# Routing the last two items each by itself, with hand-written order tables for the end of the attention stage

## The reference

```
xc   = x[b] @ W[cat_ids[b]] + b[cat_ids[b]]
x2   = xc + attention(layernorm(xc)) @ Wproj
flat = layernorm(x2)                                # 4096 x 256
gates = softmax(flat @ Wgate)                       # 8 experts
top 2 experts of each token, at most 1024 tokens per expert,
   places given out in the order of the tokens      # a running count
out  = x + x2 + sum over the two experts of gate * (gelu(rows @ W1 + b1) @ W2 + b2)
```

## Time and profile before

| | |
|---|---|
| median of 3 runs | 1525.67 us (1525.51 to 1526.84) |
| the profiled execution | 1527.01 us |
| its span, first to last instruction | 1525.2 us |
| mean granted TensorE clock | 0.957 of full |
| busy share PE, DVE, ACT, POOL | 91%, 68%, 59%, 47% |
| instructions | 27526 |

### The profile page before, as it was taken

One profiled execution on the slowest core, in us unless ns is written; L12 is line 12 of the kernel. 1 busy time (PEld: TensorE's weight loads), 2 busy tenths in 40 slices (PEclk: granted clock), 3 DMA queues, 4 the chain that ended last, 5 costly groups with the idle time before them and its releaser, 6 DMA issues.

```text
span 1525.2 us, 27526 instructions
## 1 busy us (share of the span) xinstructions
PE 1392.3 (91%) x9776; PEld 1221.8 (80%) x9776; DVE 1033.8 (68%) x2435; ACT 906.0 (59%) x2156; POOL 721.4 (47%) x720
## 2 busy tenths in 40 slices
PE   7997699999999999589999999999519999999996
PEld 5876599999999998358778777777419999998996
DVE  2999477777777775567888988895526556556552
ACT  5886255555555543158888888888526546456452
POOL 0788653444344204435465665653252435445333
PEclk9998899999999999689999999999859999999999
DMA  5421256566666614287868678686351343234212
GB/s 171 146 78 37 62 161 181 170 186 180 177 178 186 181 53 123 53 138 139 170 119 165 151 142 172 130 134 104 111 141 21 90 104 95 58 79 100 39 22 28
DMA packets 139449, 182.00 MB, mean 119 GB/s; under 512 B 22486, under 2 KB 107297, under 8 KB 139313
## 3 DMA queue, kind: packets, MB, share of 16 engines
q1 hardware_dynamic: 111152, 128.28, 33.6%
q0 software_dynamic: 28160, 51.96, 16.8%
HBM read 107.28 MB, written 42.08 MB: 98 GB/s over the span
## 4 chain that ended last, share of the span: by engine, by line
PE 78%; DVE 9%; issue 5%; POOL 3%; DMA 2%; ACT 2%; SPq 1%; POOLq 0%; DVEq 0%; ACTq 0%
PE banks L921 50%; PE banks L1365 5%; PE banks L1322 5%; PE banks L1412 3%; PE banks L440 3%; PE banks L983 2%; PE banks L1378 2%; PE banks L1339 2%; DVE lane_at L504 1%; PE banks L1759 1%; PE banks L1426 1%; DVE X L1561 1%; POOL table L1314 1%; PE banks L1346 1%; PE banks L1337 1%
## 5 line engine op out<-in xcount | busy, mean ns | idle before, releaser
L921 PE MATMUL banks<-hi_x,hi_w 128*128 128x320 f32 (+1 forms) x832 | 286.8, 345 | 10.7 <-DVE hidden L956 5.1
L921 PE MATMUL banks<-lo_x,hi_w 128*128 128x320 f32 (+1 forms) x832 | 285.6, 343 | 0.0
L921 PE MATMUL banks<-hi_x,lo_w 128*128 128x320 f32 (+1 forms) x832 | 285.2, 343 | 0.0
L921 PE MATMUL banks<-hi_w,hi_h 128*128 128x256 f32 x896 | 260.2, 290 | 2.1 <-DVE X L1010 1.7
L921 PE MATMUL banks<-lo_w,hi_h 128*128 128x256 f32 x896 | 253.5, 283 | 0.0
L921 PE MATMUL banks<-hi_w,lo_h 128*128 128x256 f32 x896 | 253.5, 283 | 0.0
L863 POOL DMA_INDIRECT xe<-pooled,idx x160 | 156.3, 977 | 198.6 <-PE banks L983 149.2
L1746 POOL DMA_INDIRECT out<-X,tab x64 | 106.5, 1664 | 204.7 <-DVE X L1843 190.1
L1459 ACT ACTIVATE PN<-banks,smax 128x256 f32<-128x256 f32 (+1 forms) x512 | 180.3, 443 | 15.9 <-DVE smax L1553 15.9
L921 PEld LDWEIGHTS banks<-hi_x,hi_w 128*128 128x128 f32 x832 | 158.3, 190 | 24.3 <-issue 10.4
L921 PEld LDWEIGHTS banks<-hi_w,hi_h 128*128 128x128 f32 x896 | 171.2, 191 | 3.3 <-issue 1.3
(11 more groups left out here) (186 smaller groups left out, 3051.4 us busy)
## 6 DMA issues: line engine op xcount, KB each, us to landing
w<-in_L_ffn_w SPq DMA_DIRECT2D x96, 256.0 KB, 5.8
done<-res SPq DMA_DIRECT2D x32, 640.0 KB, 3.9
QS<-parts_qk SPq DMA_DIRECT2D x128, 128.0 KB
KS<-parts_qk SPq DMA_DIRECT2D x128, 128.0 KB, 8.1
BIG<-in_L_ffn_W SPq DMA_DIRECT2D x16, 1024.0 KB, 9.6
mask<-in_c_masks SPq DMA_DIRECT2D x16, 257.0 KB, 2.8
pooled<-XF SPq DMA_DIRECT2D x16, 256.0 KB, 3.2
WS<-in_L_cond_W SPq DMA_DIRECT2D x16, 256.0 KB, 5.7
```

Source lines behind the costliest of these rows:

```text
L921: last = e.matmul(o, a[i], b[j], start=start and k == 0, stop=stop and k == 2, skip_group_check=True)
```

## The change

It does five things. (1) The groups get sizes: `Routing` takes a list, and group 7 is now item 14 alone, group 8 item 15 alone (2 tiles, 4 table writes each); layer 0 keeps 8 groups of 4 tiles. (2) `rounds` runs the tables only up to i = 15, and then a second table per engine, written out by item number (`PE_LAST` and so on). (3) The first two experts' matrices are loaded on SP before the stores of items 14 and 15's last results. (4) ACT and DVE begin to split matrix 0 when their attention work is done, without waiting for the slots, X and the small vectors, and SP loads those vectors ahead of the table. (5) The first product of a unit waits for the first column half alone, and loads of later matrices wait for the transposes of a unit, too.

```diff
-    r1 = Routing(region, "1", E1, K1, 0, CAP1, base1, w_pick1, slot1)
+    r1 = Routing(region, "1", E1, K1, 0, CAP1, base1, w_pick1, slot1, [R] * (NGR - 1) + [TB] * GB)
...
     def act_exp(e, r, g, logits):
-        for q in range(R):
+        for q in range(r.sizes[g]):
...
+    LAST_ROUND = B
+    PE_LAST = (
+        ("scores", 15, 3, 0), ("turn_p", 15, 2, 2), ("scores", 15, 3, 1), ("values", 15, 1), ("turn_p", 15, 2, 0),
+        ("turn_p", 15, 2, 1), ("gate_turn", 14), ("scores", 15, 3, 2), ("values", 15, 2), ("gate", 14),
+        ("turn_p", 15, 3, 2), ("rank", 14), ("turn_p", 15, 3, 0), ("turn_p", 15, 3, 1), ("values", 15, 3),
...
+    SP_LAST = (
+        ("base", 13), ("normed", 14), ("load_w1", 0), ("load_w1", 1), ("base", 14), ("normed", 15), ("base", 15))
...
-        for i in range(-4, B + 4):
+        for i in range(-4, LAST_ROUND):
             for step, off, *d in table:
                 b = i + off
-                if 0 <= b < B + (step in ROUTING):
+                if 0 <= b < B:
                     yield step, b, tuple(d)
+        for step, b, *d in last:
+            yield step, b, tuple(d)
+
+    def group_begun(b):
+
+        return b // GB if b % GB == GB - 1 and b < B - GB else NGR - 1 + b - (B - GB) if b >= B - GB else None
+
+    def group_ended(b):
+        return group_begun(b - 1) if b > 0 else None
...
             elif step == "base":
-                if b == B - 1:
-                    e.wait_ge(s_s[2], NG * B)
-                    for n in range(2):
-                        sp_load_w1(e, n)
                 e.wait_ge(s_base, b + 1)
                 e.dma_start(out_v[:, TB * b:TB * b + TB, :], X[:, TB * b:TB * b + TB, :]).then_inc(s_base_out, 16)
+            elif step == "load_w1":
+                e.wait_ge(s_s[2], NG * B)
+                sp_load_w1(e, b)
...
     def sp_experts1(e):
         wait_attn(e)
-        for q in range(NXN):
-            e.wait_ge(s_xn_out[q], 16 * (B // NXN))
-        e.wait_ge(s_base_out, 16 * B)
+        e.dma_start(b1s[:, :, :], io["b1_cols"]).then_inc(s_e1_in, 16)
+        e.dma_start(lng1[:, :, :], io["ln_cols"]).then_inc(s_e1_in, 16)
         e.wait_ge(s_scat1, 16 * NT * K1)
         e.dma_start(tab[:, :, :, :], table1.rearrange("(e p i) w -> p e i w", e=E1, p=P)).then_inc(s_tab, 16)
-        e.dma_start(b1s[:, :, :], io["b1_cols"]).then_inc(s_e1_in, 16)
-        e.dma_start(lng1[:, :, :], io["ln_cols"]).then_inc(s_e1_in, 16)
...
             elif step == "load_w1":
                 e.wait_ge(s_w1_lo, NWQ * (u - 1))
+                e.wait_ge(s_t1_ps, DC * (NH * (u - 2) + 1))
                 sp_load_w1(e, u)
...
                 if d == 0:
                     e.wait_ge(s_w1_lo, NWQ * (n + 1))
-                    e.wait_ge(s_x1_lo, DC * (u + 1))
...
                 for c in range(DC):
+                    if d == 0:
+                        e.wait_ge(s_x1_lo, DC * u + c + 1)
...
     def act_experts1(e):
-        wait_attn(e)
-        e.wait_ge(s_e1_in, 32)
+        e.wait_ge(s_lg1, B)
         for step, u, d in experts1_order():
+            if step == "turn" and u == 0:
+                wait_attn(e)
+                e.wait_ge(s_e1_in, 32)
```

More of the change, by code:

```diff
@@ L181, in __init__, with tiles @@
             self.count_steps = 2 if groups else 1
+        def tiles(self, g):
+            return sum(self.sizes[:g]), self.sizes[g]
     def dve_top(e, r, g, logits):
@@ L213, in dve_choose @@
                 yield
-            for q in range(R):
+            for q in range(n):
                 e.wait_ge(st.sem, st.n)
@@ L1169, in _build @@
         ("base", -3), ("weights", 2), ("stack", 1, 0), ("stack", 1, 1), ("normed", -2))
-    ROUTING = ("route_shift", "route_exp", "route", "rank", "place", "entry")
-    def rounds(table):
-        for i in range(-4, B + 4):
+    LAST_ROUND = B
[3 more added lines that the diff above has]
+        ("turn_p", 15, 3, 2), ("rank", 14), ("turn_p", 15, 3, 0), ("turn_p", 15, 3, 1), ("values", 15, 3),
+        ("outputs", 15, 0), ("outputs", 15, 1), ("out_turn", 15), ("proj", 15), ("rank", 15), ("gate_turn", 15),
+        ("gate", 15), ("rank", 16))
@@ L1196, in copied, with group_logits @@
                 "outputs": (s_at, TB * b + t + 1), "out_turn": (s_atT, b + 1), "proj": (s_xr, b + 1),
-                "gate_turn": (s_h2T, DC * (b + 1)), "gate": (s_lgs, b + 1), "rank": (r1.s_placed, b // GB)}[step]
-    light_uses = [a for a in rounds(PE_ROUND) if a[0] not in ("scores", "turn_p", "values")
-                  and (a[0] != "rank" or pair_ends(a[1]))]
+                "gate_turn": (s_h2T, DC * (b + 1)), "gate": (s_lgs, b + 1), "rank": (r1.s_placed, (group_ended(b) or 0) + 1)}[step]
+    def group_logits(g):
+        t0, n = r1.tiles(g)
+        return lgs[:, t0 % R * E1:(t0 % R + n) * E1].rearrange("p (r e) -> p r e", r=n)
+    light_uses = [a for a in rounds(PE_ROUND, PE_LAST) if a[0] not in ("scores", "turn_p", "values")
+                  and (a[0] != "rank" or group_ended(a[1]) is not None)]
     light_bank = {a: LBANK + i % 2 for i, a in enumerate(light_uses)}
@@ L1229, in sp_attn @@
             e.dma_start(dst, src).then_inc(s_attn_in, 16)
-        for step, b, d in rounds(SP_ROUND):
+        for step, b, d in rounds(SP_ROUND, SP_LAST):
             if step == "stack":
@@ L1281, in pool_attn @@
         begun = False
-        for step, b, d in rounds(POOL_ROUND):
+        for step, b, d in rounds(POOL_ROUND, POOL_LAST):
             if step != "got" and not begun:
@@ L1306, in pool_attn @@
                                 ALU.add).then_inc(s_base, 1)
-            elif step == "entry" and pair_ends(b):
-                g = b // GB - 1
+            elif step == "entry" and group_ended(b) is not None:
+                g = group_ended(b)
+                t0 = r1.tiles(g)[0]
                 if d[0] == 0:
@@ L1443, in pe_attn @@
                 last.then_inc(s_lg1, 1)
-            elif step == "rank" and pair_ends(b):
-                pe_rank(e, r1, b // GB - 1, bank)
+            elif step == "rank" and group_ended(b) is not None:
+                pe_rank(e, r1, group_ended(b), bank)
     def act_attn(e):
@@ L1449, in act_attn @@
         e.wait_ge(s_attn_in, N_ATTN_IN)
-        for step, b, d in rounds(ACT_ROUND):
+        for step, b, d in rounds(ACT_ROUND, ACT_LAST):
             if step == "exp":
@@ L1624, in dve_attn @@
                     next(choice, None)
-            elif step == "place" and pair_ends(b):
-                dve_place(e, r1, b // GB - 1, light_bank["rank", b, ()])
-                picked(e, r1, b // GB - 1)
-                dve_slots(e, r1, b // GB - 1)
+            elif step == "place" and group_ended(b) is not None:
+                dve_place(e, r1, group_ended(b), light_bank["rank", b, ()])
+                picked(e, r1, group_ended(b))
+                dve_slots(e, r1, group_ended(b))
     region = ExitStack()
```

124 lines of the change are left out of this document (70 added, 54 removed).

## The result

The changed kernel ran in 1517.84 us (median of 5 runs, 1517.50 to 1518.79), the kernel before, in five runs, in 1526.84 us. The ratio is 0.9945, interval 0.993 to 0.9959: 8.4 us faster (6.3 to 10.7). The direction was as forecast. The time was forecast at 1514.0; it lies 3.8 us above that, and 0.34 us above the range. The profiled execution took 1517.50 us with a span of 1515.6 us, 9.6 us less than before.

What follows compares the result with a forecast made beforehand. PE's idle hole before the full last stage, filled by table writes, read-back and gathers, was taken as the bound. Terms summed to -11.7 us, profiled 1515.3; less 1.34 to the median, forecast 1514.0, range 1510.8 to 1517.5.

Steps and rivals of the forecast that it cites:

- (a): POOL's queue: item 15's power stands behind group 6's eight table writes and starts 0.6 us late.
- (b): Addition into X on POOL now runs beside DVE's scale for item 15: +0.95 us, 0 if they miss each other.
- (c): Routing of item 15 with 2 tiles instead of 4: -1.55 us together.
- (d): Last batch of table writes on POOL: starts 2.46 us sooner, and four writes instead of eight give -5.11 us.
- (e): DVE's splits of matrix 0 move beside the last writes: +0.95 us there, -0.95 for gathers; matrix loads stay hidden.
- (f): Unit 0's gathers without a matrix load beside them: landing in 3.4 us instead of 6.12, -2.7; other end 0.
- (g): Unit 0's first product needs only the first column half, three matmuls go early: -1.42 us; other end 0.
- 1: Rival: unit 0's gathers stay slow from scattered rows, not the load; -9.0 us, time 1516.7; chance 0.12.
- 2: Rival: DVE is ahead of POOL at the scale, or the power's 0.6 us delay is absent; 1512.4 to 1513.0; chance 0.10.
- 3: Rival: stores or splits, not the table, end PE's idle hole; gain under 3 us, 1523 to 1526; chance 0.03.
- 4: Rival: later matrix loads, bound to transposes, come late and PE waits at six experts; 1526 and more; chance 0.03.

Runs made afterwards that it cites:

- the run with all amendments: Changed kernel with item 15's power ahead of two writes, DVE's splits behind the table writes, warm matmuls and filled gaps on PE; 1510.59 us, ratio 0.9895.
- the run with the power ahead: Changed kernel with the last two of group 6's eight table writes moved behind item 15's power on POOL; ratio 0.989 to the kernel before.
- the free matrix load: Changed kernel with the third matrix load no longer waiting for unit 0's transposes; ratio 0.995 to the kernel before.

## Why the prediction was right in its mechanism and wrong in its number

The chain up to the fourth product was right in its order and its waits: -11.93 us between the two first traces, -11.7 summed. That the two are so near is partly luck. In the second trace of the kernel before the fourth product starts at 60.47 from the row maximum, in the three of the changed kernel at 49.50, 49.56 and 49.82, so the same difference is 10.7 to 11.9 us. By its steps, in the first traces:

- (a) The power stood behind the eight writes: 0.46 us late (0.6 said). With two writes behind it instead, it came 0.08 us behind the variance again (the run with all amendments). When the variance itself is late by chance, as in the changed kernel's second trace, the writes delay nothing.
- (b) The scale took 0.93 us more (0.95 said), with POOL ahead by 0.08 us. Moving the addition off it gave 0.73 again (the run with the power ahead). That DVE waits out POOL's addition agrees with what the Trainium skill ("SBUF — State Buffer", Who interferes with whom) says of the shared pair of ports.
- (c) The routing of two tiles took 1.76 us less, not 1.55.
- (d) The first write of the last batch came 2.78 us sooner (2.46 said).
- (e) Three writes were slowed, not two: the four starts spanned 5.20 us, not 4.79. The gathers went at 3.84, as said. The matrix loads' place, costed at nothing, is worth 1 us by one trace, in which the last write took 1.6 us longer to land with the 4 MB issued behind item 15's rows.
- (f) The gather landed in 3.08 us (3.4 said). But in the kernel before it took 6.12 us in one trace, where it started 0.75 us ahead of the load, and 3.74 in the other, where it was 1.35 ahead. The term is worth 0.6 to 3 us by chance, and I took the first trace for the rule: its size was luck, its mechanism not.
- (g) The early products gave 1.3 us at the fourth product. At the twentieth, the mean distance from the transposes is 12.2 us in five traces where the first product waits for both halves (11.4, 11.9, 12.3, 12.4, 13.0) and 11.0 in nine where it waits for one (10.4 to 11.7): 1.2 of the 1.42 said, with a scatter as large as itself.

Two steps of the sum failed, and both stand behind the chain. The first is "PE begins products near 1127.5 instead of 1139.2, and everything after it is shifted". The products began at 1127.62, but what came after was not shifted by as much: the clock stands between the first product and the rest, and the sum had no term for it. It rose 2.70 us behind the first product in the trace that I had, the earliest of the five traces of that order (2.7, 4.0, 4.4, 4.8, 5.7), and 6.02 in the changed kernel's first. Where the first product waits for one half alone, products run without a pause from the fourth on, and the clock rose 1.9 to 4.9 us behind that in nine traces. What moves it isn't known; no run separated program from chance. That is 1.36 us of the miss. Another 0.91 was the drift ahead of the changed part: the row maximum lay at 1079.23 and 1082.64 in the kernel before and at 1080.14 and 1078.92 in the changed one, so it is chance. The second step, and the largest part with 1.7 us, is "the median of the runs lies 1.34 us below the profiled one". I took that from three runs; with two runs more that median was 1526.84, and the changed kernel's median lies 0.34 above its profiled execution. The range was short because it added bounds of single terms and had none for the clock, the drift or the reference, although the three runs before already lay 1.3 us apart. (Its bounds are also summed loosely: no wait in (a) and (b) and no slowing of the writes give 1511.5, not 1511.0. That changed nothing.)

On the later chip, with the kernel before at 1527.42 us, the same program was 12.1 us faster (9.8 to 14.5), where the sum had said 11.7. That is near the sum, but it doesn't bear it out: the medians there are 11.2 us apart, and the intervals of the two comparisons overlap only from 9.8 to 10.7. The traces agree with that overlap: from the row maximum to the end the kernel before took 445.97 and 445.96 us, the changed one 435.46, 436.04 and 435.08. So the changed part is worth 9.9 to 10.9 us, 0.8 to 1.8 less than summed, and what the times differ by beyond that lies outside this stretch.

Of the rivals, 1 is refuted by the free matrix load. Of 2, the half without contention on the scale is refuted by the trace, and the half without the 0.6 us came about in the changed kernel's second trace, but with a late variance and so without gain. 3 and 4 did not come: PE is busy 300.00 of 300 us from 1140 to 1440, and from the twentieth product to the end both kernels take the same time, so the loads of later matrices cost nothing.

## What to carry to other kernels

A hole on a chain of scatter, read-back and gather is shortened by making its last batch small: four table writes behind the last item's routing instead of eight behind two items' were worth 7 of 10.5 us by the traces. When steps of POOL are moved to make room for this, look at which of them then stands in front of the one on the chain (0.5 us here), and which of DVE's steps will run beside it (0.9 us on the scale, 1.4 on the writes). And a sum from one profiled execution needs, besides the bounds of its terms, one for what varies between executions ahead of it and for PE's clock behind every idle stretch; here these were 1 to 2 us each, as much as several terms together. Two traces of the kernel before would have shown it: they differ by 3.4 us in where the row maximum lies, by 2.7 us between slots and transposes, and by 2.1 us in the clock's rise.

## What the runs showed of the hardware that was not expected

- 24 warm matmuls ahead of the transposes shortened these (1.09 us instead of 1.94) but did nothing for the products, since the clock fell again in 2.1 us of idle time; with 12 more in the gaps it stayed at 1.00. The clock's loss in unit 0 is then 2.0 us on average (twentieth product 9.0 instead of 11.0 us behind the transposes).
- A DVE operation of 32 columns with two inputs in SBUF took 1.97 us when a table write and the addition ran on POOL, and DVE's splits made POOL's indirect writes take 1.28 to 1.50 us instead of 0.98, its gathers 1.48 instead of 0.98. The Trainium skill ("SBUF — State Buffer", Who interferes with whom) infers that such an operation doesn't hold up the making of descriptors; here POOL's indirect DMA instructions took 0.3 to 0.5 us longer each beside it. Whether that lies in the making of the descriptors or in another part of these instructions, no run separates.
- In item 15's last projection the clock may fall by chance: eight matmuls took 3.75 us in the second trace of the kernel before, at a granted clock of 0.50, and 1.97 in the first, at 1.00. It puts the power at 16.2 instead of 14.5 us from the row maximum.
